# Two transformer layers in one kernel: small products and router at other slots, three sums on VectorE

## The reference, cut to what matters

```
xn = layernorm(x)
x  = x + attn0(xn) + fp4_ffn(xn)      # layer 0
xn = layernorm(x)
x  = x + linear_attn(xn) + moe(xn)    # layer 1

attn0: 16 heads of 8; rope on q, k; softmax(q k / sqrt(8) + bias, causal)
       elastic = relu(probs + tau[h] / (row + 1))      # ALL 512 columns
       out = (elastic @ v) @ Wo.T
fp4_ffn: x, weights and the hidden rounded to FP4 in blocks of 16;
         h = silu(xq @ wg.T) * (xq @ wu.T);  out = hq @ wd.T
linear_attn: q, k = elu(rope(.) * s) + 1; causal running sum of k v^T and of k
moe: router softmax over 4 experts, top 2; 4 experts and a shared one,
     each silu(x @ sg.T) * (x @ su.T) @ sd.T, hidden 344
```

## Time and profile before

| | us |
|---|---|
| median of three runs | 2108.49 |
| profiled execution, its own time | 2108.19 |
| span of its trace | 2106.2 |
| one steady frame, from one first score pair to the next | 124.87 |
| from the start to the first score pair | 42.50 |
| from the end of the last attention frame to the end | about 97 |

### The profile page before, as it was taken

The page is one execution under the profiler, slowest core; times in us unless marked ns, Lnnn a source line. Parts: engine busy times, 40 slices in busy tenths (PEclk is TensorE's granted clock), DMA queues, the critical chain, the costliest instruction groups (busy, mean ns, idle before and its releaser), DMA issues.

```text
span 2106.2 us, 49813 instructions
## 1 busy us (share of the span) xinstructions
PE 1934.5 (92%) x17353; PEld 1264.0 (60%) x17353; DVE 1540.6 (73%) x5223; ACT 1375.7 (65%) x3861; POOL 1143.8 (54%) x1799
## 2 busy tenths in 40 slices
PE   3789999999999999999999999999999999998978
PEld 1455666656566575666657566575656657565645
DVE  6558778687776868778687877868777686876646
ACT  1677585675857667585766858567685766757531
POOL 4676374655637465473746647475563746545220
PEclk9779999999999999999999999999999999999999
DMA  5102021110301102020210201121030110201010
GB/s 146 27 9 44 4 39 23 34 29 8 54 4 38 24 20 42 4 56 6 39 24 18 44 4 39 23 39 24 10 52 4 38 24 17 40 4 34 4 32 6
DMA packets 172653, 59.37 MB, mean 28 GB/s; under 512 B 139643, under 2 KB 169971, under 8 KB 172403
## 3 DMA queue, kind: packets, MB, share of 16 engines
q1 hardware_dynamic: 172403, 56.19, 13.9%
HBM read 14.22 MB, written 4.19 MB: 9 GB/s over the span
## 4 chain that ended last, share of the span: by engine, by line
PE 56%; ACT 16%; DVE 12%; POOL 8%; issue 7%; DMA 1%; SPq 0%; ACTq 0%; DVEq 0%; POOLq 0%
PE ps L1124 11%; PE ps L1260 8%; PE ps L1195 8%; PE ps L1205 7%; ACT ring L946 5%; PE ps L1138 5%; PE ps L1114 4%; ACT pb L955 3%; PE ps L1245 3%; DVE ring L577 3%; PE ps L1183 2%; DVE lin L609 2%; POOL ring L843 2%; PE ps L1103 2%; PE ps L1171 2%
## 5 line engine op out<-in xcount | busy, mean ns | idle before, releaser
L843 POOL TENSOR_SCALAR ring<-ring,row_rcp,tau_row 128x128 f32<-128x128 f32 (+3 forms) x1024 | 625.5, 618 | 676.1 <-DVE row_rcp L584 676.1
L946 ACT ACTIVATE ring<-ring,neg_max 128x128 f32<-128x128 f32 (+3 forms) x1024 | 570.8, 558 | 504.0 <-DVE neg_max L577 499.4
L1124 PE MATMUL ps<-identf,ring 128*128 128x128 f32 x2560 | 378.6, 287 | 10.4 <-POOL ring L843 7.6
L955 ACT ACTIVATE pb<-ps 128x512 f32<-128x512 f32 x640 | 348.0, 583 | 27.5 <-PE ps L1124 23.2
L1124 PEld LDWEIGHTS ps<-identf,ring 128*128 128x128 f32 x2560 | 279.2, 143 | 83.4 <-issue 39.0
L577 DVE CUSTOM_DVE_ANT_1 ring<-ps,bias_t 128x384 f32<-128x384 f32 (+1 forms) x496 | 286.7, 614 | 53.7 <-PE ps L1114 46.4
L1260 PEld LDWEIGHTS ps<-ed_t,h 128*128 128x128 f32 (+1 forms) x1920 | 254.6, 191 | 97.2 <-issue 93.7
L1260 PE MATMUL ps<-ed_t,h 128*128 128x128 f32 (+1 forms) x1920 | 270.6, 277 | 0.0
L1205 PE MATMUL ps<-xn1T,eu_t 128*128 128x512 f32 (+1 forms) x480 | 256.5, 616 | 1.3 <-DVE h L633 1.2
L1195 PE MATMUL ps<-xn1T,eg_t 128*128 128x512 f32 (+1 forms) x480 | 255.6, 614 | 2.2 <-DVE h L626 2.1
L1114 PE MATMUL ps<-qkT 32*128 32x128 f16 (+3 forms) x1024 | 201.4, 308 | 47.1 <-DVE neg_max L577 28.0
(11 more groups left out here) (152 smaller groups left out, 2815.7 us busy)
## 6 DMA issues: line engine op xcount, KB each, us to landing
x_t<-x SPq DMA_DIRECT2D x16, 256.0 KB, 2.9
x<-x SPq DMA_DIRECT2D x16, 256.0 KB, 2.9
o_rows<-o_stack SPq DMA_DIRECT2D x256, 16.0 KB
out<-x SPq DMA_DIRECT2D x16, 256.0 KB, 2.3
qkT<-qkx SPq DMA_TRANSPOSE x128, 3.2
bias_t<-bias SPq DMA_DIRECT2D x1, 1536.0 KB, 7.8
eg_t<-eg SPq DMA_DIRECT2D x1, 860.0 KB
eu_t<-eu SPq DMA_DIRECT2D x1, 860.0 KB
```

The source lines that it names most:

```text
L843: pool.tensor_scalar(e, e, row_rcp[:, m % 2, r:r + 1], tau_row[:, i, HG * g + r:HG * g + r + 1], ALU.mult, ALU.add).then_inc(p_ok.sem, 1)
L946: act.activation(e, e, ACT.Exp, bias=neg_max[:, n % 2, r:r + 1], scale=-1.0, accum_out=row_sum[:, n % 2, r:r + 1]).then_inc(exp_ok.sem, 1)
L955: act.activation(pb[:, c % NPB, :], bank(turn_bank(q)), ACT.Relu).then_inc(t_taken[q % 2].sem, 1)
L1124: last = pe.transpose(o[:, r * P:(r + 1) * P], ring_of(i, r)[:, k * P:(k + 1) * P], idf)
```

## The change

The sum of later tokens leaves TensorE: "fx" (six small matmuls, L1148, and a copy, L592) is gone, and VectorE computes it in slot 7 (`SUM_X`) from the turned xnT, with one reduce over 384 columns into three, and two additions of one column, each after the one before. The copy of xq over xnT waits for the reduce. "fv" and "fy" move from slots 61 and 63 to slots 3 and 5 of the next frame.

In layer 1 the three "kv" go from slots 29, 29, 31 to 33, 47, 53; the turn of q ("q32") from 30 to 46; the router from slots 28 and 31 to 37 to slots 34 and 37 to 43. The down products of expert 1 start in slot 44 instead of 42, of expert 2 in slot 49 instead of 48, the others where they were; `accumulate` of experts 0, 1, 2 goes from slots 39, 46, 52 to 43, 48, 53.

In layer 0, from the second sequence on, `stack_high` goes from slots 10, 11, 12, 13 to 10, 14, 15, 18, `stack_low` and the DMA follow one and two slots behind. The four turns of the quantized hidden go from slots 11, 13, 13, 15 to 11, 15, 15, 17, and stand ahead of everything of `beside` in them; VectorE's first product of gate 1 (slot 14) overwrites the part of `hid` that is turned second (`gate_out_free`), so it now waits for a turn of slot 15.

```diff
-TURN_X, FUTURE_X, QKV0, TURN_XQ = 5, 5, 7, 10
+TURN_X, SUM_X, QKV0, TURN_XQ = 5, 7, 7, 10
-TURN_H, FUTURE_V, FUTURE_Y = (ATT + 11, ATT + 13, ATT + 13, ATT + 15), ATT + 61, ATT + 63
+TURN_H, FUTURE_V, FUTURE_Y = (ATT + 11, ATT + 15, ATT + 15, ATT + 17), ATT + 67, ATT + 69
-KV, TURN_Q32 = (L1 + 29, L1 + 29, L1 + 31), L1 + 30
+KV, TURN_Q32 = (L1 + 33, L1 + 47, L1 + 53), L1 + 46
-ROUTER = L1 + 31
+ROUTER = L1 + 37
-DOWN1 = [GATE1[3 * e + 2] + 4 for e in range(NE - 1)] + [L1 + 65]
+DOWN1 = [L1 + p for p in (35, 44, 49, 56, 65)]
+ADD_EXPERT = [L1 + p for p in (43, 48, 53, 60, 69)]
-TURN_STACK0, TURN_STACK1 = QKV0 + 5, QKV1 + 8
+TURN_STACK1 = QKV1 + 8
+STACK0 = ((10, 11, 12, 13), (10, 14, 15, 18))
...
+                if p == SUM_X:
+                    q, v = plan.turn["x", b, 0], x_future[:, b % 2, :]
+                    dve.wait_ge(t_taken[q % 2].sem, q // 2 + 1)
+                    if has(b - 2):
+                        dve.wait_ge(s_ps.sem, plan.score["fv", b - 2, 0] + 1)
+                    dve.tensor_reduce(v, xnT[:, P:L].rearrange("p (t n) -> p t n", n=P), AX_X, ALU.add).then_inc(xs_ok.sem, 1)
+                    dve.wait_ge(xs_ok.sem, xs_ok.at(b, 1))
+                    dve.tensor_tensor(v[:, 1:2], v[:, 1:2], v[:, 2:3], ALU.add).then_inc(xs_ok.sem, 1)
+                    dve.wait_ge(xs_ok.sem, xs_ok.at(b, 2))
+                    dve.tensor_tensor(v[:, 0:1], v[:, 0:1], v[:, 1:2], ALU.add).then_inc(xs_ok.sem, 1)
...
-                    if p == DOWN1[e] + 4:
+                    if p == ADD_EXPERT[e]:
                         accumulate(b, e)
...
-                if 0 <= p - QKV0 - 4 < T:
-                    stack_low(b, 0, p - QKV0 - 4)
+                if p - 1 in STACK0[b > 0]:
+                    stack_low(b, 0, STACK0[b > 0].index(p - 1))
...
                 if p == TURN_XQ:
+                    act.wait_ge(xs_ok.sem, xs_ok.at(b, 1))
                     turned(("xq", b, 0), xqT[:, :])
-                if 0 <= p - QKV0 - 3 < T:
-                    stack_high(b, 0, p - QKV0 - 3)
+                if p in STACK0[b > 0]:
+                    stack_high(b, 0, STACK0[b > 0].index(p))
...
-                for name, t in at((("hid", TURN_H),), p):
-                    turn_hidden(b, t)
...
                 for b, p in plan.beside(f, s):
+                    if p in TURN_H:
+                        for k in range(T):
+                            if TURN_H[k] == p:
+                                turn_hidden(b, k)
+                for b, p in plan.beside(f, s):
                     beside(b, p)
```

More of the change, by code:

```diff
@@ L119, in __init__ @@
                 self.turn[("probs",) + blk] = len(self.turn)
+            for b, p in self.beside(f, s):
+                for k in range(T):
+                    if TURN_H[k] == p:
+                        self.turn["hid", b, k] = len(self.turn)
             for b, p in self.beside(f, s):
@@ L163, in build @@
 def build(nc, x, wq, wk, wv, wo, bias, tau, tau_col_in, wg, wu, wd, wqkv1, wout1, eg, eu, ed,
-          cos, sin, ident, tri, inv_row, inv_col, head_mask, head_of, suffix, sel, lower, out):
+          cos, sin, ident, tri, inv_row, inv_col, head_mask, head_of, sel, lower, out):
     NB = x.shape[0]
@@ L317, in build @@
         elu_ok = signal("elu_ready", T)
+        xs_ok = signal("later_tokens_summed", T - 1)
         s_ps = signal("scores_in_psum")
@@ L341, in build @@
         first = [(identf[:, :], ident), (wqkv0_t[:, 0:D], wq), (wqkv0_t[:, D:2 * D], wk), (wqkv0_t[:, 2 * D:], wv),
-                 (cos_t[:, :, :], cos), (sin_t[:, :, :], sin), (suffix_t[:, :, :], suffix)]
+                 (cos_t[:, :, :], cos), (sin_t[:, :, :], sin)]
         fp4_weights = []
@@ L450, in _ @@
                         load(b + 1)
-                    if 0 <= p - TURN_STACK0 < T:
-                        turn_stack0(b, p - TURN_STACK0)
+                    if p - 2 in STACK0[b > 0]:
+                        turn_stack0(b, STACK0[b > 0].index(p - 2))
                     if 0 <= p - TURN_STACK1 < T:
@@ L590, in from_scores @@
                 dve.wait_ge(s_ps.sem, q + 1)
[L591 to L593 removed]
+                if name == "fv":
                     dve.tensor_tensor(v_future[:, :, :], src[:, 0:T - 1].unsqueeze(2).broadcast_to([P, T - 1, H]),
@@ L1042, in _ @@
                         store_o(b, STEPS[m][0])
+                for b, p in plan.beside(f, s):
+                    if p in TURN_H:
+                        for k in range(T):
+                            if TURN_H[k] == p:
+                                turned(("hid", b, k), hqT[:, k, :, :].rearrange("p c n -> p (c n)"), 3 * P)
                 for b, p in plan.beside(f, s):
@@ L1142, in into_scores @@
             def into_scores(b, name, k):
-                if name == "fx":
-                    pe.wait_ge(xn_ok[0].sem, xn_ok[0].at(b, T))
+                if name == "fv":
                     o = score_ticket((name, b, k))
-                    for j in range(1, T):
-                        last = pe.matmul(o[:, 0:T - 1], xn[:, j, :], suffix_t[:, j, :], start=(j == 1), stop=(j == T - 1))
-                elif name == "fv":
-                    o = score_ticket((name, b, k))
-                    pe.wait_ge(s_taken.sem, plan.score["fx", b, 0] + 1)
+                    pe.wait_ge(xs_ok.sem, xs_ok.at(b, T - 1))
                     last = pe.matmul(o[:, 0:T - 1], wqkv0_t[:, 2 * D:3 * D], x_future[:, b % 2, :], start=True, stop=True)
@@ L1341, in shape_constants @@
         head_mask[HD * h:HD * (h + 1), h, :] = 1
-    suffix = np.zeros((P, T, T - 1), f)
-    for j in range(T):
-        suffix[:, j, 0:j] = 1
     sel = np.zeros((P, HG, NV), f)
@@ L1354, in shape_constants @@
         "inv_row": np.broadcast_to(f(1) / (pos + 1), (P, L)), "inv_col": (f(1) / (pos + 1)).reshape(T, P).T,
-        "head_mask": head_mask, "head_of": head_of, "suffix": suffix, "sel": sel, "lower": lower,
+        "head_mask": head_mask, "head_of": head_of, "sel": sel, "lower": lower,
     }
```

6 lines of the change are left out of this document (2 added, 4 removed).

## The result

| | before | changed |
|---|---|---|
| median, us | 2108.76 (4 runs) | 2179.66 (2178.66 to 2182.27, 4 runs) |
| span of the trace, us | 2106.2 | 2176.8 |
| shortest steady frame, us | 124.86 | 128.74 |
| mean of 13 steady frames, us | 124.91 | 129.76 |
| mean granted clock | 0.981 | 0.970 |

The changed kernel is slower: ratio 1.0339, interval 1.0321 to 1.0357. The forecast was 2140, with a range to 2160: the direction was right, the size less than half. In the changed kernel the lines are: scores L1132, turn of probabilities L1142, gate and up of layer 1 L1208 and L1218, down L1273, kv L1175, lin L1184, bias L583, exponential L960, hidden's copies L926, stacks L950/951 and L849/850, GpSimd's scaling L857.

What follows compares the result with a forecast made beforehand. The prediction took a chain of waits across engines as the bound, TensorE itself only in slots 32 to 61. Its terms, 0.3 + 0 + 1.9 = 2.2 us a frame, 33 us over fifteen frames, gave 2140 us, range 2098 to 2160.

Steps and rivals of the forecast that it cites:

- (a): Frame's end to slot 20: earlier start, sums in slot 7, moved stacks and hidden's turns; +0.3 us a frame.
- slower still: Rival: GpSimd holds an addition in slot 7 for 0.43 to 1.27 us, +0.9 a frame, about 2155 us; chance 0.15.
- that tanh comes 0.4 later: Gate 3's tanh on ScalarE, behind stack 3 in slot 18, was to come 0.4 us later than before.
- the whole 0.4 + 0.6: ScalarE's added work ahead of gate 3's tanh: fourth hidden copy in slot 17 (0.4 us), stack 3 in slot 18 (0.6).
- The bounds: Limits for (a): -0.9 us if the norm's gain is kept and ScalarE's move covered, +1.0 at the other end.
- (b): Slots 21 to 31: the kv, router steps and turn of q that leave are not on the chain; cost 0.
- the faster rival: VectorE truly bounds slots 21 to 31; relieving it brings slot 32's turn about 2 us forward, about 2091 us; chance 0.24.
- TensorE comes to slot 32 earlier and waits there. Cost 0: Slots 21 to 31: with small products gone, TensorE only waits longer before slot 32's turn, at no cost.
- the pause of 1.32 us: TensorE's wait before the third kv; up to that much would be gained if the chain carried it.
- (c): Slots 32 to 61, TensorE nearly always busy: kv 0.85, turn of q 0.49, moved down tile 0.6; +1.9 us a frame.
- What would show it: Signs: frame about 127 us, y_future off the chain, GpSimd releasing slot 32, gate 3's tanh later, slot 43's span near 2.3 us.
- the sum's 33: The forecast's total over fifteen frames at 2.2 us each: 33 us.

Runs made afterwards that it cites:

- e4: The changed kernel with the three sums as three reduces (384, 256 and 128 columns) instead of one reduce and two additions: 2165.69 us, 1.0260 against the kernel before.
- e2: The kernel before with, of the change, only layer 0's stacks in slots 10, 14, 15, 18 and the hidden's turns in 11, 15, 15, 17: 2124.32 us, ratio 1.0065.
- e12: The kernel before with the sums as three reduces on VectorE in slot 7, and fv and fy in slots 3 and 5: 2103.60 us, ratio 0.9973.
- e8: The kernel before with only the sum of later tokens moved to VectorE, as three reduces in slot 7; fv and fy stay: 2106.89 us, ratio 0.9985.
- e7: The kernel before with, of the change, only the router, the down products of experts 1 and 2 and the accumulates moved: 2125.43 us, ratio 1.0069.
- e3: The kernel before with only layer 1's part of the change (kv, turn of q, router, down products, accumulates): 2162.74 us, ratio 1.0244.
- e5: e3 with sixteen transposes that nobody reads added to TensorE in slot 30 of layer 1's sequence: 2141.67 us, 1.0147 against the kernel before.
- e15: e3 with the three kv products left in slots 29, 29 and 31, the turn of q in slot 46: 2139.75 us, 1.0139 against the kernel before.

## Why the prediction was wrong, step by step

- **(a) The frame's start, forecast +0.3, measured +1.86 a frame: 28 us for 15 frames instead of 5 (its own terms end at a tanh 0.4 us late, the sum takes 0.3).** Two terms were mis-sized. The sums: 0.85 to 0.9 us forecast, 2.0 measured, since the second addition is held by GpSimd, and 1.01 of it reaches slot pair 8. I had this as the rival "slower still" at 0.43 to 1.27 us and gave it 0.15; the row that spoke for it, shows a GpSimd instruction of 1.27 us in that very slot, the single executions of L666 would have spoken for it too, and e4 shows that it was so. The stacks and turns: "that tanh comes 0.4 later" after taking off 0.3 and 0.3 of gain. By themselves they cost 1.01 (e2), the whole 0.4 + 0.6 with nothing to take off for slots 13 to 16; and the gain from before them came to 0.16 (e12 against e8 is 0.19) where I took 0.3: the chain did leave `y_future` and the frame's end, pairs 60 and 62, is 1.40 shorter, but slots 0 to 5 take 1.27 of it back. The bounds, -0.9 to +1.0, were too narrow.
- **(b) Slots 21 to 31, forecast 0.** As a matter of waits it held: slot 32 is released by GpSimd as before, pairs 28 to 32 together are +0.18 with the "kv" of slot 33 in them, and e7 shows that VectorE's relief gives nothing. So the faster rival fell. The step "TensorE comes to slot 32 earlier and waits there. Cost 0" failed in a way that I had not named at all: waiting costs clock. It is 21 us in e3 against e5 and 13 in the steady frames of the changed kernel. I had read the pause of 1.32 us as something to gain, and not asked what a longer one does.
- **(c) Slots 32 to 61, forecast +1.9, measured +1.81 (e5, pairs 34 to 62).** The sum is right by two errors; some luck is in that. Router and experts cost 0.95 where I had 0.6: the accumulation in slot 43 with the last router steps, put at 0 to 0.3, costs 0.82; the tile taken out of slot 43 gains 0.29 and not 0.1 (from the "lin" at 1096.76 to the step behind the scores at 1099.14 is 2.38 us before, 1103.67 to 1105.76 is 2.09 in e7); and the step behind slot 42's scores comes after 0.64 us and not 0.88, which no term had. The small products cost 0.89 and not 1.34: the turn of q 0.40 (e15 against e7), the kv's of slots 47 and 53 0.25 and 0.24, and the third falls into slot 33, ahead of these pairs.
- **What would show it.** The frame is 128.7 to 131.2, not 127. Slot 32's releaser (with 0.83 us of wait of TensorE before it, where the kernel before has under 0.1), the chain's way out of the old frame and the span behind the "lin" of slot 43 (2.1 us, near 2.3) came as said. So did the tanh of gate 3: it begins 1.50 us ahead of layer 1's first q/k/v product, 2.03 in the kernel before, and the second of these products now waits 0.38 us for gate 3's.

The span grew by 70.6 us. To the sum's 33, (a) adds 23, pairs 28 to 32 add 3 and the low clock of the thirteen steady frames 13; (c) takes 1 off, and nothing is left for the fill, the drain and the low clock outside these frames, which cancel.

## What to carry to other kernels

A pause of TensorE is not free for being off the path: where small products are taken out of one, look up how much idle time the stretch then has, and leave them, or put work for nobody there. Before two-input additions go onto VectorE, look at what GpSimd does in that slot; a reduce that reads twice the columns can be the cheaper instruction. When a stretch gets shorter, follow which instruction it pushes beside which: of 1.40 us gained at the frame's end 0.13 to 0.19 arrived.

## What the runs showed of the hardware

- Sixteen useless transposes (1.97 us) in a pause of 2.46 us made a kernel 21 us faster (2162.7 to 2141.7), with the granted clock at 0.978 instead of 0.971.
- The low clock did not need a long standstill: 2.46 us of pause and 0.8 a little later, with a gate product and a score pair between, were enough in 8 of 13 steady frames of e3, while with 1.3 us (the kernel before) and 1.5 us (e7) as the longest pause the clock fell there in none.
- An addition of one column took 1.22 us beside a GpSimd instruction that had begun 0.08 us earlier, and 0.26 beside one that had 0.25 us left; both ended within 0.02 us of GpSimd's. A two-input instruction of 16 columns (the router's) took 0.17 us with nothing of GpSimd beside it, and 0.52 to 0.68 where it began 0.11 to 0.26 us behind a scaling that reads SBUF. A TENSOR_SCALAR of 32 columns, with one SBUF input, took 0.85 to 0.86 in place of 0.27 to 0.30, and ended within 0.04 us of GpSimd's instruction.
